# A new order of the steps in a hybrid attention and feed-forward block on one core

## The reference

```python
x = x + attn_a(layernorm(x), Wqkv, bqkv, Wo, bo)    # one head of 128
x = x + ffn(layernorm(x), qweight, scale, zero, bias)
x = x + attn_b(layernorm(x), wq, wk, wv, wo)        # 32 heads of 16, rotary, causal
x = x + ffn(layernorm(x), qweight, scale, zero, bias)

# attn_a: softmax(q k^T / sqrt(128)) v Wo + bo
# attn_b: rotary on q and k, scores where key > query are masked,
#         softmax over 256 keys, probabilities times v, times wo
# ffn:    weight = (int4 nibbles - zero) * scale;  input @ weight^T + bias
```

## Time and profile before

| | us |
|---|---|
| median of 3 runs | 275.57 (275.15 to 275.82) |
| the profiled execution, whole | 276.74 |
| its span, first to last instruction | 275.0 |
| TensorE busy | 253.9 (92%) |
| VectorE busy | 230.1 (84%) |
| GpSimd busy | 185.8 (68%) |
| ScalarE busy | 143.7 (52%) |

### The profile page before, as it was taken

The page is one execution under the profiler, slowest core; times in us unless marked ns, Lnnn a source line. Parts: engine busy times, 40 slices in busy tenths (PEclk is TensorE's granted clock), DMA queues, the critical chain, the costliest instruction groups (busy, mean ns, idle before and its releaser), DMA issues.

```text
span 275.0 us, 6466 instructions
## 1 busy us (share of the span) xinstructions
PE 253.9 (92%) x2295; PEld 210.0 (76%) x2295; DVE 230.1 (84%) x416; ACT 143.7 (52%) x237; POOL 185.8 (68%) x226
## 2 busy tenths in 40 slices
PE   5698989899997999978999999999999999998994
PEld 2586867696896988866887888798878787685774
DVE  2587968588997999996999889799799989796896
ACT  5347797646247146544533475844455654456330
POOL 3277889999998967595557858545878454437371
PEclk9999999999999999999999999999999999999999
DMA  6999562003463535333432333444344433102104
GB/s 173 299 387 380 214 215 57 0 0 83 122 170 108 146 107 152 109 110 108 137 113 75 101 99 96 119 133 118 104 121 117 134 99 100 58 3 79 39 0 153
DMA packets 52151, 33.94 MB, mean 123 GB/s; under 512 B 5592, under 2 KB 46744, under 8 KB 52120
## 3 DMA queue, kind: packets, MB, share of 16 engines
q1 hardware_dynamic: 52120, 33.54, 40.6%
HBM read 25.00 MB, written 8.39 MB: 121 GB/s over the span
## 4 chain that ended last, share of the span: by engine, by line
PE 41%; POOL 23%; SPq 13%; issue 7%; DMA 6%; DVE 6%; ACT 2%; POOLq 0%; ACTq 0%; DVEq 0%
SPq L522 11%; PE psum L954 7%; PE psum L955 6%; PE psum L956 6%; POOL X L596 6%; POOL wb_lo L601 5%; PE psum L1133 5%; POOL rstd L577 4%; PE psum L1096 4%; PE psum L1118 3%; PE psum L1048 3%; DMA QK<-qk_parts 2%; PE psum L1049 2%; PE psum L978 2%; DMA qk_parts<-parts 2%
## 5 line engine op out<-in xcount | busy, mean ns | idle before, releaser
L623 POOL TENSOR_SCALAR_AFFINE_SELECT E<-E 128x512 f32<-128x512 f32 x64 | 41.7, 676 | 41.2 <-ACT E L766 41.1
L903 DVE TENSOR_REDUCE nmax<-psum 128x4 f32<-128x512 f32 (+1 forms) x64 | 59.2, 943 | 4.5 <-PE psum L1096 4.2
L766 ACT ACTIVATE E<-psum 128x1536 f32<-128x1536 f32 x32 | 46.3, 1447 | 22.9 <-PE psum L1120 17.4
L954 PE MATMUL psum<-XT_lo,wb_hi 128*128 128x256 f32 x128 | 37.9, 296 | 0.0
L630 ACT ACTIVATE parts<-SH 128x512 bf16<-128x512 f32 x32 | 20.0, 627 | 32.4 <-POOL SH L612 21.8
L955 PE MATMUL psum<-XT_hi,wb_lo 128*128 128x256 f32 x128 | 36.2, 282 | 0.0
L956 PE MATMUL psum<-XT_hi,wb_hi 128*128 128x256 f32 x128 | 36.1, 282 | 0.0
L954 PE MATMUL psum<-wb_lo,XT_hi 128*128 128x256 f32 (+1 forms) x96 | 32.4, 337 | 0.6 <-DVE XT_lo L834 0.6
L1096 PE MATMUL psum<-QK 128*128 128x128 bf16 x256 | 28.8, 220 | 2.2 <-DMA QK<-qk_parts 2.2
L955 PE MATMUL psum<-wb_hi,XT_lo 128*128 128x256 f32 (+1 forms) x96 | 30.6, 319 | 0.0
L956 PE MATMUL psum<-wb_hi,XT_hi 128*128 128x256 f32 (+1 forms) x96 | 30.6, 319 | 0.0
(11 more groups left out here) (119 smaller groups left out, 674.2 us busy)
## 6 DMA issues: line engine op xcount, KB each, us to landing
QK<-qk_parts SPq DMA_DIRECT2D x192, 64.0 KB
qk_parts<-parts SPq DMA_DIRECT2D x16, 384.0 KB, 2.8
X<-L_attn_a_x SPq DMA_DIRECT2D x8, 256.0 KB, 7.9
out<-X SPq DMA_DIRECT2D x6, 256.0 KB, 2.2
wb_raw<-L_attn_b_wq SPq DMA_DIRECT2D x1, 1024.0 KB, 10.0
wb_raw<-L_attn_b_wk SPq DMA_DIRECT2D x1, 1024.0 KB, 12.8
wb_raw<-L_attn_b_wv SPq DMA_DIRECT2D x1, 1024.0 KB, 14.7
QK<-mask_rows SPq DMA_DIRECT2D x8, 128.0 KB
```

The lines of the kernel that those rows point to most:

```text
L623: last = nc.gpsimd.affine_select(out=e, in_=e, compare_op=ALU.is_ge, fill=0.0, base=0, pattern=[[0, GH], [1, P]], channel_multiplier=-1)
L766: nc.scalar.activation(E[:, n % 2], bank(3, 3), ACT.Exp, scale=float(HD) ** -0.5).then_inc(done[k], 1)
L903: nc.vector.tensor_reduce(nmax[:, u % 2, g::NG, t], (bank(1, 2) if t else bank(0)).rearrange("p (h k) -> p h k", h=GH), AX, ALU.max, negat ...
L954: nc.tensor.matmul(out_, stat[0], mov[1], start=first, stop=False)
```

## The change

Only the list `PLAN` changes. The new one has the same steps but for one: `("KP", 5, 0)`, the five idle matmuls in the tail, is gone. Every other step stands in it once, most of them at another place, and code that reads the list (bank turns, slots of XN and XT, which waits count to what) follows it. The reordered list is long, so here are its parts around the steps that the prediction speaks of. Lines of "..." leave out the rest.

```diff
-    ("D", "xt", 1, 0), ("D", "wqkv", 0), ("D", "xt", 0, 0), ("XH", 1, 0), ("XL", 1, 0), ("QH", 0), ("QL", 0), ("KP", 8),
-    ("D", "wqkv", 1), ("D", "bqkv"), ("XH", 0, 0), ("XL", 0, 0), ("QH", 1), ("QA", 0, 0, 0), ("QA", 0, 1, 0),
...
-    ("D", "xt", 0, 3), ("XH", 0, 3), ("D", "x", 0, 1), ("XL", 0, 3), ("CS",), ("D", "wo1"), ("BM",), ("CE",),
-    ("D", "xt", 0, 2), ("XH", 0, 2), ("QA", 0, 1, 1), ("LN", 1, 0, 1), ("QS",), ("RS", 1, 0), ("D", "bias_o"),
-    ("XL", 0, 2), ("QA", 0, 1, 2), ("QA", 0, 1, 3), ("BO",), ("BA", 1, 0, 0), ("D", "x", 1, 0), ("Z", 0, 1),
...
+    ("D", "xt", 1, 0), ("XH", 1, 0), ("XL", 1, 0), ("D", "wqkv", 1), ("QH", 1), ("D", "wqkv", 0), ("QH", 0), ("KP", 8),
+    ("QL", 1), ("D", "wqkv", 2), ("QH", 2), ("D", "xt", 0, 0), ("D", "xt", 0, 1), ("QL", 0), ("XH", 0, 0), ("XL", 0, 0),
+    ("D", "x", 0, 0), ("LN", 1, 0, 0), ("XH", 0, 1), ("QA", 1, 0, 0), ("XL", 0, 1), ("D", "xt", 0, 2), ("QL", 2),
+    ("XH", 0, 2), ("QA", 1, 1, 0), ("QA", 0, 1, 0), ("D", "wqkv", 3), ("XL", 0, 2), ("D", "x", 0, 1), ("LN", 1, 0, 1),
+    ("RS", 1, 0), ("D", "x", 1, 1), ("QH", 3), ("QL", 3), ("D", "bqkv"), ("QA", 0, 1, 1), ("D", "x", 1, 0),
+    ("LN", 1, 1, 1), ("LN", 1, 1, 0), ("QS",), ("BC",), ("D", "xt", 1, 1), ("D", "wo1"), ("QA", 0, 1, 2), ("XH", 1, 1),
+    ("XL", 1, 1), ("D", "xt", 0, 3), ("D", "bias_o"), ("QA", 0, 0, 0), ("QA", 0, 0, 1), ("CS",), ("XH", 0, 3), ("BM",),
+    ("XL", 0, 3), ("CE",), ("RS", 1, 1), ("QA", 0, 0, 2), ("BO",), ("BA", 1, 0, 0), ("BA", 1, 0, 1), ("BA", 1, 1, 1),
...
-    ("P2", 1), ("P3", 1), ("RS", 2, 3), ("RP", 2), ("PJ", 3, 0), ("SS", 0), ("BA", 2, 2, 1), ("PJ", 3, 1), ("RO", 3),
...
-    ("P3", 2), ("BA", 2, 2, 0), ("SS", 1), ("VV", 0), ("S", 0, 0, 1), ("FS", 2, 2, 1), ("QM", 3), ("RS", 3, 1),
-    ("NO", 3, 1, 0), ("T", 3, 1, 0), ("FS", 2, 2, 0), ("MX", 0, 0, 0), ("S", 0, 1, 0), ("NO", 3, 1, 1), ("SL", 1),
...
-    ("SS", 2), ("VV", 1), ("BA", 2, 3, 0), ("PJ", 4, 0), ("P2", 3), ("P3", 3), ("SS", 3), ("S", 1, 0, 0),
...
+    ("RS", 3, 1), ("NO", 3, 1, 1), ("MX", 0, 0, 1), ("LN", 2, 3, 1), ("BA", 2, 2, 1), ("S", 0, 1, 0), ("S", 0, 1, 1),
...
+    ("FS", 2, 2, 1), ("P3", 3), ("FS", 2, 2, 0), ("RS", 2, 3), ("PJ", 4, 0), ("SL", 1), ("FD", 2, 2, 1), ("PJ", 4, 1),
+    ("S", 1, 0, 0), ("S", 1, 0, 1), ("RO", 4), ("PJ", 5, 0), ("SL", 2), ("NO", 2, 3, 1), ("BA", 2, 3, 1),
+    ("NO", 2, 3, 0), ("PJ", 5, 1), ("T", 2, 3, 1), ("T", 2, 3, 0), ("SS", 3), ("MX", 1, 0, 0), ("SM", 0),
...
+    ("LN", 3, 2, 0), ("SS", 4), ("FS", 2, 3, 1), ("R1", 5), ("P2", 5), ("EX", 0, 0), ("ON",), ("PJ", 6, 1), ("RO", 6),
...
+    ("NO", 4, 0, 1), ("MT", 6), ("M1", 6), ("MX", 7, 0, 0), ("P3", 9), ("ST", 5, 1), ("S", 7, 1, 0), ("S", 7, 1, 1),
+    ("NX", 4), ("RO", 11), ("M2", 6), ("RP", 11), ("T", 4, 0, 1), ("NO", 4, 0, 0), ("SS", 9), ("VP", 4, 0),
...
+    ("PV", 13, 1), ("ST", 14, 0), ("EX", 14, 0), ("VP", 7, 0), ("MX", 15, 1, 0), ("MT", 15), ("M1", 15), ("RS", 4, 2),
+    ("NO", 4, 2, 0), ("FS", 4, 1, 1), ("M2", 15), ("MK", 14, 0), ("VP", 7, 1), ("VV", 7), ("NA", 13), ("ST", 14, 1),
+    ("PV", 14, 0), ("EX", 14, 1), ("T", 4, 2, 0), ("TH", 4, 2, 0), ("SM", 15), ("ST", 15, 0), ("BA", 4, 2, 0),
...
-    ("FS", 4, 3, 0), ("FD", 4, 2, 1), ("FD", 4, 3, 0, 0), ("KP", 5, 0), ("T", 4, 3, 1), ("TH", 4, 3, 1),
...
+    ("F", 4, 3, 0, 0), ("FS", 4, 3, 0), ("NO", 4, 3, 1), ("BA", 4, 3, 1), ("T", 4, 3, 1), ("TH", 4, 3, 1),
+    ("FD", 4, 2, 1), ("OS", 2, 1), ("FD", 4, 3, 0, 0), ("TL", 4, 3, 1), ("RW", 4, 3, 1), ("FS", 4, 3, 1),
```

## The result

The median fell from 275.69 us (4 executions, 275.15 to 278.07) to **268.82 us** (4, 268.69 to 269.07): -6.9 us, ratio 0.9736, 95% interval 0.968 to 0.979. The forecast was -2.5 us, 273.1, range 270.0 to 277.6. The direction was right, the size was not.

A forecast was written before the change was run, and what follows sets the result against it. The prediction saw a kernel near balance (TensorE, GpSimd, SyncE), with open TensorE waits before 130 us to win. Terms -3.6 -2.8 -0.5 +0.6 +2.0 +1.8 = -2.5 us took the median 275.57 to 273.1 us, range 270.0 to 277.6.

The forecast's parts named there:

- Norms: GpSimd's normalisation steps: moved ahead of other GpSimd work, they spare TensorE's transposes waits; -3.6 us, lower bound of gain 1.9.
- The five waits: Five TensorE transposes wait 4.3 us in all for a normalised tile, the longest 1.90 us at T 3 1 0.
- Stacks in the middle: SyncE's queue: SL 2 ahead of SS 3 removes about 5 us of dead time; -2.8 us, bound -1.4.
- Stacks late: SS 13 and SS 14 ahead of SL 12 and SL 13 remove the wait at S 15 0 0; -0.5 us, bounds 0 and -0.8.
- Start: First loads: wo1 lands 2.5 to 3.0 us later, mostly hidden by earlier matmuls; +0.6 us, bounds -1.5 and +1.5.
- Row maxima: Units 6 and 15: VectorE steps between MT and M2 make the maxima late for TensorE; +2.0 us, bounds 0 and 4.
- rival of late maxima: Less TensorE cover in eleven of sixteen units, a quarter showing as waits for row maxima; 278.0 us, slower, chance 0.17.
- Exponentials: ScalarE: EX 0 0, EX 4 1 and EX 5 0 behind a waiting P2, each costing at least 0.63 us; +1.8 us, range 0 to 5.4.
- KP: Idle matmuls removed from the tail: VectorE's ten last steps stay full and the same; 0 us, bounds -0.3 and +0.3.
- clock rival: Without the idle matmuls the last four half products could run at 1.2 GHz; plus 1.9 us, 275.0 us, chance 0.04.
- Better: Rival: loads on time and no wait for row maxima; 269.0 us, chance 0.08.
- Absorbed: Rival: VectorE is the true bound from 90 to 130 us, so TensorE's waits there only move; 275.4 us, chance 0.12.

The follow-up runs named there:

- b_norm: Kernel before with the one step RS 3 1 moved ahead of BA 2 2 0: 279.2 us, ratio 1.013, all six executions below full clock.
- h97: New order up to PJ 6 1 (396 steps), old order for the rest: 270.6 us at full clock, ratio 0.980 to before.
- h57: New order up to PJ 0 0 (227 steps), old order for the rest: 274.9 us at full clock, ratio 0.998 to before.
- o90: Old order up to T 2 3 1 (352 steps), new order for the rest: 274.1 us at full clock, ratio 0.993 to before.
- a_m2: Kernel after with M2 6 and M2 15 right behind M1 and SM 15 behind M2 15: 270.8 us at full clock, ratio 0.984 to before.
- a_ex: Kernel after with EX 0 0, EX 4 1 and EX 5 0 put ahead of the P2 before them: 268.4, 269.8 and 270.9 us, ratio 0.977 to before.
- h97_nokp: New order up to PJ 6 1, old order for the rest, without the idle matmuls in the tail: 271.0 us.
- b_stack: Kernel before with the one step SL 2 moved ahead of SS 3: 273.4 us at full clock, ratio 0.993.
- a_unstack: Kernel after with the one step SL 2 moved back behind SS 3: 269.4 us at full clock, ratio 0.976 to before.
- a_rs31: Kernel after with RS 3 1 and NO 3 1 1 moved behind BA 2 2 1: 269.5 us, ratio 0.978 to before.
- a_kp: Kernel after with the five idle matmuls put back ahead of T 4 3 1: 269.8 us, ratio 0.977 to before.
- h31: New order up to T 2 0 1 (147 steps), old order for the rest: 275.9 us at full clock, ratio 1.001 to before.
- o133: Old order up to S 6 0 0 (525 steps), new order for the rest: 275.9 us at full clock, ratio 1.006 to before.
- h57_stack: New order up to PJ 0 0, old order for the rest, with SL 2 ahead of SS 3: 273.1 us at full clock.
- h90: New order up to T 2 3 1 (352 steps), old order for the rest: 277.2 us, no execution at full clock, ratio 1.003 to before.
- h133: New order up to S 6 0 0 (525 steps), old order for the rest: 270.9 us at full clock, ratio 0.979 to before.
- o57: Old order up to PJ 0 0 (227 steps), new order for the rest: 272.1 us at full clock, ratio 0.986 to before.
- a_free: Kernel after with the M2, SM 15 and three EX steps all put back to early places: 273.3 us at full clock, ratio 0.992 to before.

## Why the prediction was wrong

The measured time lies below the stated range. The steps that failed are the costs that I booked, +4.4 us in all (start 0.6, row maxima 2.0, exponentials 1.8), of which the runs show none, and the place where I looked for the gain of the norms. Term by term:

**Norms, forecast -3.6: right in sign, put at the wrong place.** The five waits went. But the step by which RS 3 1 loses at least 5.2 us of GpSimd work against a wait of 1.90 us saw one wait where there was a chain: GpSimd almost without a gap from 49 to 83 us, busy 32.5 of these 34 us. RS 2 1 starts at 51.3 in after (57.7 before), T 2 1 1 at 57.0 (61.1), F 2 1 0 at 65.0 (71.6), LN 3 1 1 at 71.2 (79.1), and only so is RS 3 1 early: before, LN 3 1 1 ended at 80.0 and RS 3 1 began at 80.8, so its own move could win 0.8. b_norm, which moves this one step and leaves the other three, shows that alone it wins nothing. The size by subtraction: h97 less h57 is 4.3 us; less 1.9 for SL 2, 2.4 remain. That subtraction is an argument, not a run.

**Stacks in the middle, forecast -2.8: -1.9 alone, in before.** The term was too large by 0.9 and inside its bound. That the one step brings the gain is shown. Of the step "about 5 us of dead time leave the queue" the traces show 4.9 us at SL 2, 2.0 at SL 3 and none at SL 4. In after the same place is worth 0.6.

**Stacks late, forecast -0.5.** The 0.55 us at S 15 0 0 are gone in after. No run has this alone. The order behind 97 us gives 1.8 us in all (270.6 to 268.8), of which the run with KP back leaves 0.8.

**Start, forecast +0.6: none that stands out.** QT 0 came at 17.3 to 18.3 us in the six traces with the old start (median 17.6) and at 16.9 to 19.6 in the fourteen with the new one (median 17.8). The mis-sized term is "it lands 2.5 to 3.0 us later" for wo1, and with it the 2.08 us that BM waits in the earlier trace rows. In the profiled execution of before wo1 landed at 13.4, but in the five other traces with the old start at 10.9 to 11.7, and BM did not wait there. In the fourteen with the new start it was issued at 7.4 to 7.8, for 6.0, and landed at 12.6 to 13.7. So by medians it lands 1.8 us later, 0.4 of it between issue and landing, and the cover of 2.1 us that I counted hides that. The wait of BM was this one execution's, and its removal isn't a gain of the order. BM and the landing of wo1 in o90, which has the old start:

```profile
11.04 0.59 PE L987 MATMUL psum<-wo,TR 128*128 128x512 f32 x1
```

```profile
DMA to landing us min/median/max: 4.9/4.9/4.9
```

In the trace of before it took 7.4 us, in that of after 5.6. There BM started at 14.6, behind CS and without a wait.

**Row maxima, forecast +2.0: 0.** No ST waits for one. The step that failed is "MX, P3, NX and RO now stand between MT and M2", booked with 3.3 us. It started VectorE's queue at MT's end; three of the four ran before it. In unit 6 the maxima were in place some 0.7 us before ST 6 0 (SM 6's issue ended at 156.5, plus the 1.9 of the earlier trace rows, against 159.1). The other way round, a_m2 shows the places that I had called early to cost 1.9 us. My rival of late maxima fell with it.

**Exponentials, forecast +1.8: no cost in the trace, and a_ex leaves the size open.** The failing step is "each costs at least the P2 itself". P2 8 ended at 139.0 as ST 4 1 did. P2 5 held EX 0 0 for some 0.6 us, and its reader PV 0 0 came only at 104.4. P2 9 held nothing up: it started after a gap of 1.7 us, but EX 5 0 behind it waited another 0.25 us for TensorE's PV 4 0, and its own reader, PV 5 0, came only at 159.9:

```profile
148.91 0.63 ACT L629 ACTIVATE parts<-SH 128x512 bf16<-128x512 f32 x1 [1.68 <-POOL SH L615]
149.80 1.45 ACT L765 ACTIVATE E<-psum 128x1536 f32<-128x1536 f32 x1 [0.25 <-PE psum L1132]
```

**KP, forecast 0: 0 in the old tail, -1.0 in the new one.** I claimed that VectorE's ten last steps are full and the same. They are the same, but FD 4 2 1 starts 2.8 us behind the end of WO 3 1 1 in after and 3.2 in h97_nokp, and once it is early KP is the next limit. The clock rival didn't come: no execution of after was below 0.998.

**The sum.** The three gains stood at -6.9, and the measured change is -6.9, or -6.5 against the many later executions at full clock. None of the +4.4 of booked costs appeared. That the gains then match is luck: by the runs two of them were too large (2.4 for 3.6 and 1.9 for 2.8), and KP (1.0) and the first 57 us (0.4 alone) made up for them. The rival "Better" (0.08, 269.0) comes nearest in number. It was right that the loads cost nothing at QT 0 and that no row maximum is waited for, but it kept my three gains and the +1.8 of the exponentials. The larger error is of method: I priced each move at a consumer on TensorE. Single steps, moved either way, gave +1.5 at equal clock and +3.8 with the clock's part (b_norm), -1.9 (b_stack), +0.6 (a_unstack), +0.6 (a_rs31) and +1.0 (a_kp). What one of them is worth depends on the order around it: SL 2's place 1.9 us in before and 0.6 in after, KP nothing in the old tail and 1.0 in the new one, and the new first 57 us 0.4 ahead of the old rest and 3.2 ahead of the new. The rival "Absorbed" did not come: from PJ 6 1 to S 5 0 0 the lead grew from 4.8 to 6.4 us.

## What to carry to other kernels

In a kernel whose engines are nearly in balance, take the chain that ended last stretch by stretch before pricing a reordering. Here a consumer's wait of 1.9 us showed only the last link of a chain that ran through GpSimd for 34 us. A step placed late in another engine's queue costs nothing while the steps ahead of it run in the time in which its input is being made; placed right behind its producer it can hold up all of them. So compare when the queue gets there with when the input is ready. Judge a cut or a one-step edit by its seam first, since it brings new waits of its own. And take the row that a term rests on from more than one execution: the wait of 2.08 us at BM was in one trace of six.

## What the runs showed of the hardware

TensorE's clock falls after a thin stretch in mid-kernel, and near the edge it is a matter of the execution. In h31 TensorE was busy 0.78 of 2 us and the granted clock was 0.62 and 0.53 in the next two slices (0.5 is the 1.2 GHz level), and 1.00 again from 90 us on:

```profile
84.00:86.00 2.00, 0.78 (x9) 0.77 (x10) 1.21 (x2) 1.61 (x3) 1.84 (x4) 1.00 0.60 172
86.00:88.00 2.00, 2.00 (x10) 1.70 (x9) 1.45 (x3) 1.89 (x4) 1.08 (x2) 0.62 0.51 139
88.00:90.00 2.00, 2.00 (x8) 1.23 (x7) 0.54 (x1) 1.64 (x4) 2.00 (x2) 0.53 0.00 0
```

The profiled execution of before had 0.44 us busy in 82 to 84 and kept its clock; 41 of the 102 others had a lower mean clock, at a price of 2.3 us in the median. Where it fell in those no trace shows, but in the traces of b_norm, b_stack, o133, h31, h57 and h57_stack it fell between 83 and 87 us, close to the same wait, and in h90 at 98 us, behind the wait of 4.74. Of 42 executions of after, h97, h97_nokp, h133, o57, a_kp, a_rs31 and a_ex none had it. A removed wait can thus be worth more than its length, and the spread of before, 273.8 to 279.9 us, is a sign of it. It isn't enough to remove the one wait at T 3 1 0: b_norm did and had the lower clock in all six executions, with TensorE busy 2.08 of the 4 us from 80 to 84. Nor does the rest of the new order protect everywhere. 5 of 11 executions of a_free, 1 of 4 of a_m2, 1 of 6 of a_unstack and 2 of 12 of o90 had a lower mean clock, and the trace of a_free shows it at 158 us, behind a wait of 1.6 us at T 4 0 1. The Trainium skill, TensorE: Matmul & The Clock Gate, Part 1, says that the clock falls after idle time, and these rows agree; I had applied it to the tail alone.

FS 2 2 0 in b_norm took 1.73 us, from 82.61 on, against 0.74 for the same operation just before, while a GpSimd operation on tiles of 512 columns ran from 82.52 to 83.79. The Trainium skill, SBUF — State Buffer, section SBUF: two separate sides, describes such waiting as a lock on shared ports; the row agrees, and no run here separates it from another cause.
